# Row sums moved from VectorE to transfers, three of seven block rows folded by transfers, and new band sizes in a mixed-precision 3x3 convolution

## The reference, cut to what matters

```
def _predictor_mask(x):
    pooled = x.reshape(B, C, H // POOL_K, POOL_K, W // POOL_K, POOL_K).mean(axis=(3, 5))
    m = pooled >= THRESH
    ...
x_high = jnp.where(mask, x, EPS)
x_low = jnp.where(mask, EPS, x)
y_high = _conv(_quant_act_uint(x_high, act_scale_high, 8), _quant_weight_per_oc(w_high, 8))
y_low = _conv(_quant_act_uint(x_low, act_scale_low, 4), _quant_weight_per_oc(w_low, 4))
return y_high + y_low
```

## Time and profile before

| | us |
|---|---|
| median of 3 runs | 621.39 (620.23 to 621.58) |
| the profiled execution | 621.01 |
| its span (first to last instruction) | 619.3 |
| what lies around the span | 1.7 |

### The profile page before, as it was taken

How to read it: one execution, slowest core, us unless ns; L and a number is a source line. 1 busy time by engine, 2 the same in 40 slices (tenths; PEclk the granted TensorE clock), 3 DMA queues, 4 the chain that set the end, 5 groups by cost and what they waited for, 6 DMA issues and landing times.

```text
span 619.3 us, 10727 instructions
## 1 busy us (share of the span) xinstructions
PE 598.7 (97%) x3564; PEld 343.5 (55%) x3564; DVE 592.3 (96%) x727; ACT 492.6 (80%) x524; POOL 84.7 (14%) x96
## 2 busy tenths in 40 slices
PE   4898899999999999999999999999999999999996
PEld 3554455555555555555555555555555555555553
DVE  6899999999999999999999999999999999999953
ACT  6789888788888778888778888877888877888443
POOL 4330011111011111110111101111101011100000
PEclk9899999999999999999999999999999999999999
DMA  7499899888889888889988789988888988884122
GB/s 284 157 256 320 264 297 262 250 247 257 289 260 307 233 254 236 271 269 297 261 239 249 257 280 271 294 236 242 248 279 258 309 249 252 225 278 123 66 105 104
DMA packets 48010, 152.25 MB, mean 246 GB/s; under 512 B 2688, under 2 KB 30048, under 8 KB 44032
## 3 DMA queue, kind: packets, MB, share of 16 engines
q1 hardware_dynamic: 14400, 103.95, 44.0%
q0 software_dynamic: 33600, 48.17, 37.2%
HBM read 100.73 MB, written 51.38 MB: 246 GB/s over the span
## 4 chain that ended last, share of the span: by engine, by line
PE 91%; DVE 3%; ACT 3%; issue 2%; DMA 1%; DVEq 0%; SPq 0%; ACTq 0%
PE psum L387 90%; PE psum L371 1%; DVE ybuf L786 1%; ACT psum L540 1%; DMA wraw_l<-w_low 1%; ACT rounded_l L502 1%; ACT rounded_h L502 1%; DVE planes L721 1%; DVE inner L742 0%; DVE outer L757 0%; DVE pooled L692 0%; ACT shared L567 0%; DVE w_max_l L661 0%; DVE middle L779 0%; DVEq L68 0%
## 5 line engine op out<-in xcount | busy, mean ns | idle before, releaser
L540 ACT ACTIVATE psum<-psum,ratio 128x672 f32<-128x672 f32 (+2 forms) x190 | 189.6, 999 | 73.2 <-PE psum L387 70.8
L387 PE MATMUL psum<-planes,wT_l 128*128 128x336 f16 (+1 forms) x792 | 145.3, 333 | 3.5 <-DVE ybuf L786 3.4
L387 PE MATMUL psum<-planes,wT_h 128*128 128x336 f16 (+1 forms) x792 | 146.3, 334 | 0.0
L567 ACT ACTIVATE shared<-psum,bias,out_scale_h 128x448 f32<-128x448 f32 (+1 forms) x128 | 86.7, 677 | 34.8 <-PE psum L387 34.8
L387 PEld LDWEIGHTS psum<-planes,wT_l 128*128 128x128 f16 x792 | 76.9, 97 | 61.6 <-DVE ybuf L786 4.7
L387 PEld LDWEIGHTS psum<-planes,wT_h 128*128 128x128 f16 x792 | 77.2, 97 | 58.8 <-issue 1.6
L502 ACT ACTIVATE rounded_l<-xbuf,inv_act_l 128x1568 int16<-128x1568 f32 (+1 forms) x64 | 101.8, 1593 | 4.7 <-DMA xbuf<-x 4.7
L502 ACT ACTIVATE rounded_h<-xbuf,inv_act_h 128x1568 int16<-128x1568 f32 (+1 forms) x64 | 102.3, 1602 | 0.0
L350 POOL DMA_DIRECT2D halves<-x x30 | 44.8, 1493 | 369.9 <-DMA halves<-x 369.9
L387 PE MATMUL psum<-rowsums,wT_h 128*128 128x448 f16 (+1 forms) x384 | 86.6, 334 | 1.9 <-ACT wT_h L520 1.9
L387 PE MATMUL psum<-rowsums,wT_l 128*128 128x448 f16 (+1 forms) x384 | 86.0, 332 | 0.2 <-DVE rowsums L733 0.2
(11 more groups left out here) (69 smaller groups left out, 487.0 us busy)
## 6 DMA issues: line engine op xcount, KB each, us to landing
y<-ybuf SPq DMA_DIRECT2D x64, 784.0 KB, 4.7
xbuf<-x SPq DMA_DIRECT2D x31, 1568.0 KB, 9.9
halves<-x POOLq DMA_DIRECT2D x60, 784.0 KB, 12.9
xbuf<-x SPq DMA_DIRECT2D x1, 896.0 KB, 7.9
xbuf<-x SPq DMA_DIRECT2D x1, 672.0 KB, 5.2
wraw_l<-w_low SPq DMA_DIRECT2D x1, 576.0 KB, 3.9
wraw_h<-w_high SPq DMA_DIRECT2D x1, 576.0 KB, 6.2
act_scales<-scales SPq DMA_DIRECT2D x1, 1.0 KB, 1.8
```

The lines of the kernel that those rows point to most:

```text
L387: last = nc.tensor.matmul(out, wT[k][:, mat, :], moving(k, p, band, row, dx), start=(k == "l" and j == 0), stop=(j == len(parts) - 1), ski ...
L540: return nc.scalar.activation(banks, banks, ACT.Identity, scale=ratio[:, 0:1])
L567: nc.scalar.activation(shared[band % 2][:, 0:columns(band)], psum[:, BANK[band % 2]["T"], 0:columns(band)], ACT.Identity, bias=bias[:, 0:1 ...
```

## The change

Four things. (1) From image 3 on POOL makes the row sums by transfers from SBUF to SBUF: for each k one that copies the even plane into the row sums and one that adds the odd plane onto them (128 x 1626 f16 each). PE waits for their landing (`s_rows_summed`) at high and low of band 0. DVE keeps the row sums of images 0 to 2. (2) Only three of the seven block rows are folded by transfers, and from image 4 on; DVE reduces 672 numbers of `halves` and the other 1792 from x in SBUF. Images 2 and 3 are pooled from x alone (3136). (3) The bands are 8, 5, 7 and 8 pairs, before 8, 6, 6 and 8; so the fast bands hold 15 pairs, before 14, and the differences get that much longer. (4) In image 1 the inner and outer differences of image 2 stand behind out_rows 3.

```diff
-    BAND = ((0, 8), (8, 6), (14, 6), (20, 8))
+    BAND = ((0, 8), (8, 5), (13, 7), (20, 8))
...
+        FOLD = 3
+        halves = sb("halves", [P, 2, FOLD, POOL // 2 * W], F32)
...
-            def block_halves(i, p):
-
-                n = 2 * i + p
-                image = xd[bass.ds(n, 1), :, :].rearrange("b c (a h r) -> (b c) a h r", h=2, r=POOL // 2 * W)
-                pool.wait_ge(s_pooled, prepared(n - 2))
-                nc.gpsimd.dma_start(halves[p][:, :, :], image[:, :, 0, :]).then_inc(s_half, 16)
-                pool.wait_ge(s_half, 16 * (n - 1))
-                nc.gpsimd.dma_start(halves[p][:, :, :], image[:, :, 1, :], accum_op=ALU.add).then_inc(s_halves, 16)
...
+            def begin_row_sums(k, m, p):
+
+                j = "lh".index(k)
+                pool.wait_ge(s_plane[k], prepared(m))
+                nc.gpsimd.dma_start(all_rowsums[:, bass.ds(p, 1), j, :], all_planes[:, bass.ds(p, 1), j, 0:SUMS]
+                                    ).then_inc(s_rows_copied[k], 16)
+
+            def add_row_sums(k, m, p):
+
+                j = "lh".index(k)
+                pool.wait_ge(s_rows_copied[k], 16 * (m - 2))
+                nc.gpsimd.dma_start(all_rowsums[:, bass.ds(p, 1), j, :],
+                                    all_planes[:, bass.ds(p, 1), j, EVEN + PITCH:EVEN + PITCH + SUMS],
+                                    accum_op=ALU.add).then_inc(s_rows_summed[k], 16)
...
+            begin_halves(4, 0)
+            add_halves(4, 0)
+            with pool.Fori(3, B - 2) as m:
+                p = m % 2
+                begin_row_sums("l", m, p)
+                begin_halves(m + 2, p)
+                begin_row_sums("h", m, p)
+                add_row_sums("l", m, p)
+                add_row_sums("h", m, p)
+                add_halves(m + 2, p)
...
                 elif band == 0:
-                    pe.wait_ge(signal, prepared(n))
+
+                    pe.wait_ge(s_rowsum[k], prepared(2))
+                    pe.wait_ge(s_rows_summed[k], 16 * (n - 2))
...
+                if not (isinstance(n, int) and n < 4):
+
+                    dve.wait_ge(s_halves, 16 * (n - 3))
+                    nc.vector.tensor_reduce(
+                        pooled[:, 0:FOLD * BX].rearrange("p (a b) -> p a b", b=BX),
+                        halves[:, p, :, :].rearrange("p a (y b x) -> p a b y x", b=BX, x=POOL), AX.XY, ALU.add
+                        ).then_inc(s_folded, 1)
+                    a0 = FOLD
...
                     for k in "lh":
                         row_sums(k, m, mp)
-                    inner_differences(m, mp)
-                    outer_differences(m, mp)
                     out_rows(n, p, 2)
                     pool_blocks(1, 1)
                     choose(3)
                     out_rows(n, p, 3)
+                    inner_differences(m, mp)
+                    outer_differences(m, mp)
                     return
...
-                    row_sums("l", m, mp)
...
-                    row_sums("h", m, mp)
```

More of the change, by code:

```diff
@@ L83, in conv_program @@
         clipped = {k: sb(f"clipped_{k}", [P, HW], F16) for k in "hl"}
-        planes = [sb(f"planes{p}", [P, 2, PLANE], F16) for p in range(2)]
+        all_planes = sb("planes", [P, 2, 2, PLANE], F16)
+        planes = [all_planes[:, p, :, :] for p in range(2)]
         plane = {k: [planes[p][:, j, :] for p in range(2)] for j, k in enumerate("lh")}
-        rowsums = [sb(f"rowsums{p}", [P, 2, SUMS], F16) for p in range(2)]
-        rowsum = {k: [rowsums[p][:, j, :] for p in range(2)] for j, k in enumerate("lh")}
+        all_rowsums = sb("rowsums", [P, 2, 2, SUMS], F16)
+        rowsum = {k: [all_rowsums[:, p, j, :] for p in range(2)] for j, k in enumerate("lh")}
         outer = [sb(f"outer{p}", [P, 2, 2, FAST_SUMS], F16) for p in range(2)]
@@ L153, in conv_program @@
         s_rowsum = {k: sem(f"rowsum_ready_{k}") for k in "hl"}
+        s_rows_copied = {k: sem(f"row_sums_begun_{k}") for k in "hl"}
+        s_rows_summed = {k: sem(f"row_sums_landed_{k}") for k in "hl"}
         s_half = sem("upper_halves_landed")
+        s_folded = sem("folded_pooled")
         s_halves = sem("halves_landed")
@@ new lines, in add_row_sums, with image_halves @@
+            def add_row_sums(k, m, p):
[4 more added lines that the diff above has]
+                                    accum_op=ALU.add).then_inc(s_rows_summed[k], 16)
+            def image_halves(m):
+                image = xd[bass.ds(m, 1), :, 0:FOLD * POOL * W]
+                return image.rearrange("b c (a h r) -> (b c) a h r", h=2, r=POOL // 2 * W)
@@ new lines, in begin_halves, with add_halves @@
+            def begin_halves(m, p):
+                pool.wait_ge(s_pooled, prepared(m - 2))
+                nc.gpsimd.dma_start(halves[:, bass.ds(p, 1), :, :], image_halves(m)[:, :, 0, :]).then_inc(s_half, 16)
+            def add_halves(m, p):
+                pool.wait_ge(s_half, 16 * (m - 3))
+                nc.gpsimd.dma_start(halves[:, bass.ds(p, 1), :, :], image_halves(m)[:, :, 1, :], accum_op=ALU.add
+                                    ).then_inc(s_halves, 16)
+            for p in range(2):
+                pool.wait_ge(s_border[p], BORDERS)
@@ new lines, in _ @@
+            begin_halves(4, 0)
[8 more added lines that the diff above has]
+                add_halves(m + 2, p)
+            with pool.Fori(B - 2, B) as m:
+                p = m % 2
+                begin_row_sums("l", m, p)
+                begin_row_sums("h", m, p)
+                add_row_sums("l", m, p)
+                add_row_sums("h", m, p)
@@ L390, in products, with wait_prepared @@
                 return last
-            def wait_prepared(signal, n, band):
+            def wait_prepared(k, n, band):
                 if first_image(n):
-                    pe.wait_ge(signal, 1 if band == 0 else 2)
+                    pe.wait_ge(s_rowsum[k], 1 if band == 0 else 2)
+                elif band == 0 and early(n):
+                    pe.wait_ge(s_rowsum[k], prepared(n))
+                elif band == 0 and isinstance(n, int):
+                    pe.wait_ge(s_rows_summed[k], 16 * (n - 2))
                 elif band == 0:
-                    pe.wait_ge(signal, prepared(n))
+                    pe.wait_ge(s_rowsum[k], prepared(2))
+                    pe.wait_ge(s_rows_summed[k], 16 * (n - 2))
             def low(n, p, band):
@@ L400, in low @@
                 new = not (first_image(n) and band < 2)
-                wait_prepared(s_rowsum["l"], n, band)
+                wait_prepared("l", n, band)
                 if new:
@@ L430, in high @@
                 g = BANDS * n + band
-                wait_prepared(s_rowsum["h"], n, band)
+                wait_prepared("h", n, band)
                 if fast(n, band):
@@ L682, in pool_blocks @@
                 a0, a1 = (0, BY) if q is None else PART[q]
[L683 to L688, removed]
-                else:
[L690 to L693, removed]
+                if first_image(n) and q == 0:
+                    dve.wait_ge(s_x_start, 16)
+                else:
+                    dve.wait_ge(s_x[p], 16 * i + 16)
+                if not (isinstance(n, int) and n < 4):
[5 more added lines that the diff above has]
+                    a0 = FOLD
+                nc.vector.tensor_reduce(
+                    pooled[:, a0 * BX:a1 * BX].rearrange("p (a b) -> p a b", b=BX),
+                    xbuf[p][:, a0 * POOL * W:a1 * POOL * W].rearrange("p (a y b x) -> p a b y x", y=POOL, b=BX, x=POOL),
+                    AX.XY, ALU.add).then_inc(s_pooled, 1)
             def choose(n, q=None):
@@ L697, in choose @@
                 dve.wait_ge(s_pooled, prepared(n, 1 if q is None else q))
+                if not (isinstance(n, int) and n < 4):
+                    dve.wait_ge(s_folded, n - 3)
                 if not first_image(n):
```

## The result

The changed kernel takes 637.86 us (four runs, 634.53 to 641.58) where the one before takes 621.25: a ratio of 1.0247, interval 1.0203 to 1.0291. The forecast was 619.6 us, with a range of 616 to 648. The profiled execution took 634.53 us, the shortest of the four; its span is 632.8, 13.5 more than before. So the trace may show a mild case; the two runs of 641 us have none.

A forecast was written before the change was run, and what follows sets the result against it. PE was taken as the bound at 18.34 us an image, DVE close at 18.22. Start +2.3 us and 28 images at 0.146 (-4.1) gave -1.8: 619.2 us profiled, 619.6 against the median 621.39; range 616.0 to 648.

The forecast's parts named there:

- Both in time, by 1 to 2 us and by 4: Row-sum adds for PE's band 0: l lands at +16 to +17.3, h at +18 to +19, both before PE wants them.
- Rival B: Row sums land late at PE's first matmul on them in band 0, from image 3; 621 to 646 us, chance 0.23.
- the main branch: Transfer queue with issues of 0.5 to 0.6 us per row sum: add l lands by +17.3, add h by +19.
- The branch beside it: If issues cost as much as before: add l lands at +17.5, add h behind the x load at +23.3, 0.4 late.
- The copies' landing: Row-sum copy of 416 KB, time to land: 5.4 - 2.0 + 1.05 - 0.5 = 3.9 us.
- The queue's sum: DMA time of one image's x, y, folding and row-sum transfers: 17.1 us of 18.19, fitting with 1 us, at 94%.
- The price of an f16 add by bytes: Each 416 KB row-sum add in the DMA engines costs 2.1 us by bytes, not 4.2 by elements.
- rival C: f16 adds in the DMA engines cost by element: 3 us more an image, about 700 us; chance 0.17.
- PE: Matmuls of an image fall from 42336 to 42000 columns: 18.34 to 18.19 us, 0.146 us less an image.
- DVE: Without two row sums, with longer pooling, rows and differences: 18.22 - 0.6 = 17.6 us an image, under PE's 18.19.
- The start: PE waits for DVE's added pooling and moved differences in the first images; image 4 begins near 102.2, not 99.88: +2.3 us.
- POOL held off writing descriptors by DVE: DVE's two-port modes lock POOL out of descriptor writing: given nothing; by the rule up to 1.1 us per issue meeting a clip.

## Why the prediction was wrong

- **The failed step** is "Both in time, by 1 to 2 us and by 4", for h, and in its sum the landing of add h, 4.6 us, a price worked out for an add with little beside it. Rival B came in. By the forecast add h is issued at +13.4 to +14.4 (it lands at +18 to +19) and the x load at +15.3, so the load starts while the add is under way, and the main branch gave this no cost. Measured, medians of the loop: add h is issued at +14.2, the load at +15.6, and add h lands in 7.3 us, in the late images in 9.2 to 10.7. The branch beside it, not taken, had the mechanism: "add h is issued at +14.5 and comes behind the x load ... and lands at +23.3, 0.4 late". In image 9 the add was issued at +13.9 us from the start of image 8 on PE (178.38), the load at +15.5, and it landed at +24.4. That branch was tied to the issues' cost, and that was not what did it: issues took 0.57 (copy) and 0.88 us (add) where 0.5 to 0.6 were taken for both.
- **The copies' landing** was mis-sized as well, 3.9 forecast, 5.2 median measured, with the two row copies, the fold's copy and the end of a y store in flight together. Each add waits for its copy: add l is issued at +12.1 and not +11.2, and add h 2 us behind it. With two, one and no rows folded the copies land in 3.8, 2.7 and 2.7 us, the lead of add h over the load grows to 2.1 to 4.6 us, and no h sum is late.
- **The cause.** That the load's start makes the h sums late is shown: moved by 2 us with all else kept, 637.9 became 622.2 us. How the late packets and the load's come to their order within an engine is not shown.
- **The queue's sum** of 17.1 of 18.19 us measured 18.2 as a mean over the span, and 18.9 in the loop (1.01 of 492.9 us in 26.3 images); this is time that packets took, the time in each other's company included. It was taken as room for everything ("It fits with 1 us"); with the load held the share is 1.00 and PE waits 2.0 us in all, so fullness by itself cost little. What cost is which transfer is in flight when.
- **The price of an f16 add by bytes** was right, and rival C fell. In the change only packets of two adds, of l and then of h sums, are in flight here (DMA share, GB/s last), beside the earlier trace rows:

```profile
193.20:195.80 2.60, 2.60 (x16) 1.37 (x14) 2.36 (x6) 2.04 (x4) 1.29 (x1) 1.00 1.06 190
```

  190 GB/s is 2.19 us for 416 KB; 2.1 was taken, and by elements it would be 4.2. The rule of the Trainium skill ("Collectives: The Full Stack", Part 3: two sources read, no cost of adding) agrees with this row for f16: half of the 395 GB/s of copies would be 198.
- **PE** at 18.19 us an image was right: 18.19 or 18.20 in 16 of 27 images of the change and in all with two folded rows and the new bands. **DVE** at 17.6: its clips of images 4 and 5 begin at 87.50 and 105.18, 17.68 apart, while it was behind. The sum with the bands alone, 18.54, measured 18.52.
- **The start** was taken at +2.3 us and is +3.24 in the profiled execution (103.12 for image 4, 99.88 in the earlier trace rows). Images 2 and 4 begin 42.21 us apart where it was 40.84, so 1.4 us arise there and 1.9 ahead of image 2. The clock does not explain the 1.9. The mean over the first 20 us looks as if it did (the changed kernel, then the one before; PE busy, PEclk, DMA share, GB/s):

```profile
0.00:20.00 20.00, 9.84 (x84) 0.91 0.55 220
```
```profile
0.00:20.00 20.00, 9.44 (x87) 0.98 0.56 220
```

  But each of the two has one stretch of 3.4 us at 1.2 GHz ahead of image 2, behind a stretch at 2.4 GHz in which PE was busy in part (1.49 of 3.4 us, 4.72 of 6.8); in the kernel before it lies across the 20 us:

```profile
14.60:18.00 3.40, 3.40 (x11) 0.51 0.01 4
```
```profile
19.20:22.60 3.40, 3.37 (x10) 0.50 0.48 93
```

  The five kernels with row sums by transfers that have such a stretch begin image 2 at 60.2 to 60.9, and the eight without at 58.4 to 60.0. Like against like, 60.2 to 60.9 against 59.04, 1.2 us or more of the 1.9 are the change's, and the start costs about 2.6 to 3.2 us (an estimate, with the 1.4). The prediction's working for it (DVE's longer pooling of images 2 and 3) is not borne out in full: folding image 2 early left the 42.45 us as they were, and with the old bands images 2 and 4 are 41.93 apart, so the longer differences are little of it too. What sets it stays open.
- **POOL held off writing descriptors by DVE** (the Trainium skill, "SBUF — State Buffer", "Who interferes with whom"), given nothing: copies took 0.56 to 0.61 us to issue and adds 0.86 to 0.91, in all 116 of them, so nothing is what it cost here. None of the 116 ran beside a clip, as the prediction had it (clips earlier, issues later); what a clip costs an issue was therefore not tried.
- **The sum.** 619.2 was forecast for the profiled execution and 634.53 measured: 14.2 us of waits for h sums, 0.9 more at the start, 0.2 left over. Rival B's price was added up a little low: 0.1 to 1 us on 28 images, less 1.8, gives 622 to 648 and not 621 to 646; the measured time lies in both.

## What to carry to other kernels

When work moves from a compute engine to transfers, adding up bytes against the period is not enough: write out for each transfer that someone waits for when it is issued, what is in flight then, and what big load is issued close behind it (in the change and with the h copy first the late ones had the load 0.6 to 2.3 us behind). A chain of small transfers that wait for each other loses a little at each landing, and the last link meets the load; there a smaller fold gave back all of the waits, and holding the load for 2 us all but 2 us, while ordering the load strictly behind the sums cost 25 us more. Test an edit to a queue by moving the start of one transfer and keeping the bytes.

## What the runs showed of the hardware

- A 416 KB transfer over 16 engines ended at 10.4 us by one engine where fifteen were done at 5.6: packets of an x load issued 1.6 us behind it ran ahead of its last ones. That its queue was first did not protect it.
- Adding in f16 within SBUF moved 190 GB/s where only adds were in flight, about the price per byte of adding onto f32 (197 GB/s).
- Issuing 128 pieces took GpSimd 0.57 us for a copy and 0.88 for an adding transfer, 896 pieces 0.96 and 1.49.
- A DMA share of 1.01 and of 1.00 over 493 us stood beside 14.2 us of PE's waits and beside 2.0: the share alone did not tell them apart.
